# A graph-attention layer: the query projection moved from the prologue into the edge loop, ahead of the linear attention

## The reference

```
xn = layernorm(x)                                   # [6250, 256]
# 1. graph attention, 8 heads of 32, 206250 edges sorted by target node dst
q = xn @ Wq.T + bq;  k = xn @ Wk.T + bk;  v = xn @ Wv.T + bv
sim[e, h] = <q[dst[e]], k[src[e]]> / sqrt(32)
attn = softmax of sim over the edges of one dst
agg[d] = sum over its edges of attn * v[src[e]]
x1 = x + agg @ Wo.T + bo
# 2. linear attention over all nodes, 8 heads of 64
x1 += (q' @ (norm(k').T @ norm(v')) / N) @ w_out.T + b_out,   q', k', v' = xn @ w_qkv.T
# 3. a mixture of 8 experts of 1024 hidden units, each token goes to one expert
out = x1 + moe(layernorm(x1))
```

## Time and profile before

| | value |
|---|---|
| time, median of three runs | 2950.68 us |
| profiled execution: its span | 2949.1 us |
| busy share of the span: PE, DVE, ACT, POOL | 72%, 82%, 34%, 72% |
| matmuls, DVE instructions, POOL instructions | 9400, 3296, 2220 |
| granted TensorE clock, mean of the span | 0.875 |
| mean share of the 16 DMA engines, POOL's queue / SP's queue | 57.4% / 11.2% |
| first and last gather of `kv_d` rows begin | 272.61 and 2382.17 us |

### The profile page before, as it was taken

How to read it: one execution, slowest core, us unless ns; L and a number is a source line. 1 busy time by engine, 2 the same in 40 slices (tenths; PEclk the granted TensorE clock), 3 DMA queues, 4 the chain that set the end, 5 groups by cost and what they waited for, 6 DMA issues and landing times. The chain is left out here.

```text
span 2949.1 us, 36213 instructions
## 1 busy us (share of the span) xinstructions
PE 2127.7 (72%) x9400; PEld 1712.6 (58%) x9401; DVE 2429.0 (82%) x3296; ACT 1010.5 (34%) x4314; POOL 2119.7 (72%) x2220
## 2 busy tenths in 40 slices
PE   5675777767776777767888876556666655599998
PEld 4473555555565666555666554444444435599997
DVE  5676788888888999999999888899999985366665
ACT  3220555556566666611111111011111114345353
POOL 4465777777777777777777777777777775567785
PEclk9796888998999999989999898887888885599999
DMA  6746777777777777788888887777777758423331
GB/s 218 246 156 172 208 210 208 207 211 217 219 218 219 218 219 218 227 233 241 257 255 257 254 241 213 212 211 211 211 211 211 211 162 288 152 70 76 88 92 15
DMA packets 257830, 587.19 MB, mean 199 GB/s; under 512 B 49410, under 2 KB 135505, under 8 KB 257565
## 3 DMA queue, kind: packets, MB, share of 16 engines
q0 software_dynamic: 150480, 467.10, 57.4%
q1 hardware_dynamic: 97947, 109.47, 11.2%
q10 hardware_dynamic: 9296, 9.44, 0.9%
HBM read 519.05 MB, written 71.76 MB: 200 GB/s over the span
## 5 line engine op out<-in xcount | busy, mean ns | idle before, releaser
L1041 POOL DMA_INDIRECT wide<-kv_d,arena x1099 | 1051.0, 956 | 335.0 <-issue 326.7
L1340 PE MATMUL ps<-wide,arena 128*128 128x264 f32 x2432 | 694.6, 448 | 238.9 <-DVE wide L1444 238.6
L1340 PEld LDWEIGHTS ps<-wide,arena 128*128 128x128 f32 x2432 | 530.2, 223 | 395.2 <-DVE wide L1444 283.4
L1041 POOL DMA_INDIRECT arena<-kv_d,arena x539 | 515.3, 956 | 164.3 <-issue 159.1
L1176 ACT ACTIVATE ps<-wide 128x256 f32 x229 | 88.8, 388 | 1324.2 <-DVE arena L1410 1282.5
L1413 DVE TENSOR_REDUCE arena<-arena 128x64 f32<-128x2048 f32 x229 | 523.5, 2286 | 7.9
L1340 PE MATMUL ps<-arena 128*128 128x264 f32 x1216 | 350.4, 451 | 128.7 <-DVE arena L1444 128.7
L1410 DVE TENSOR_TENSOR arena<-wide,ps 128x2048 f32<-128x2048 f32 x153 | 349.3, 2283 | 105.7 <-DMA wide<-kv_d,arena 105.6
L1340 PEld LDWEIGHTS ps<-arena 128*128 128x128 f32 x1216 | 267.0, 225 | 209.0 <-DVE arena L1444 152.9
L1444 DVE TENSOR_TENSOR wide<-wide,ps 128x2112 f32<-128x2112 f32 x152 | 356.8, 2347 | 24.4 <-ACT arena L1191 24.4
L141 PE MATMUL ps<-halves 128*128 128x256 f32 (+2 forms) x2304 | 361.9, 319 | 3.2 <-DVE halves L1703 1.6
(11 more groups left out here) (310 smaller groups left out, 3137.8 us busy)
## 6 DMA issues: line engine op xcount, KB each, us to landing
wide<-kv_d,arena POOLq DMA_INDIRECT x1099, 3.8
arena<-in_w SPq DMA_DIRECT2D x16, 1024.0 KB, 5.4
kv_d<-wide SPq DMA_DIRECT2D x49, 260.0 KB, 2.2
arena<-xn_d SPq DMA_DIRECT2D x82, 128.0 KB, 3.4
arena<-kv_d,arena POOLq DMA_INDIRECT x539, 3.8
hb_d<-arena SPq DMA_DIRECT2D x16, 516.0 KB
q_d<-wide SPq DMA_DIRECT2D x49, 128.0 KB, 2.7
xn_d<-arena SPq DMA_DIRECT2D x7, 896.0 KB, 9.0
```

The costliest lines, as they stand in the source:

```text
L1041: e.indirect_dma_start(out=kvb[k][:, j, :], out_offset=None, in_=kv_d, in_offset=bass.IndirectOffsetOnAxis(ap=ixb[k][:, j:j + 1], axis=0)) ...
L1340: m = e.matmul(psE[(k + 1) % 3][:, 0:264], ident, kvb[b][:, j, 256:ROW], start=(j == 0), stop=(j == J - 1))
```

## The change

The projection of the queries leaves the prologue. In its place:

- the raw rows of `x` are copied from DRAM to DRAM into `row_d` (6250 rows of 256 numbers, `[0:N, 0:256]`), which also holds the neighbour lists (columns 256 to 319) and, in columns 320 and 321, each row's scale and offset of the layer norm, stored by `store_stat` once per group of seven tiles;
- POOL's sorted gathers (L600 for the first 13 tiles, L1171 for the other 36) bring rows of `row_d`, 322 numbers wide, instead of `q_d`. The first 13 no longer wait for the stores of k, v and q but for the lists and the scales (`t_rn`);
- `LEAD` = 3 tiles are turned into queries in straight code behind `grant`; the first eight rounds of the edge loop, 48 chunks (`CONV`), turn the other tiles into queries, one per chunk: ACT scales and shifts (`centered`), PE transposes (`turned`), ACT copies, PE multiplies (`queried`), ACT scales and writes the tile over the gathered one, SP stores it to `qs_d`. `mix`, `join` and `aux` follow behind these 48 chunks;
- the weight in the prologue has 512 columns instead of 768, and the tables are made for 294 instead of 300 chunks.

The work per tile in the prologue, and the release of the gathers (in the code T is PE, V DVE, S ACT, G POOL and Y SP; `wait(engine, tokens)` makes that engine wait):

```diff
-                    b0, b1_ = ps[2 * (u % 2)], ps[2 * (u % 2) + 1]
+                    b0 = ps[2 * (u % 2)]
                     wait(T, t_lo[u], t_bias.get(u - 2), t_W)
-                    for b_, c0, n in ((b0, 0, 512), (b1_, 512, 256)):
-                        m = product(b_[:, 0:n], [(xq[u % 2][:, i, k * 128:(k + 1) * 128], w[:, k, c0:c0 + n]) for k in range(2)
-                                                 for i, w in ((0, wh), (0, wl), (1, wh))])
+                    m = product(b0[:, 0:KV], [(xq[u % 2][:, i, k * 128:(k + 1) * 128], w[:, k, :]) for k in range(2)
+                                              for i, w in ((0, wh), (0, wl), (1, wh))])
...
+        s_xr, s_wq = sem("s_xr"), sem("s_wq")
+        dma(Y, row_d[0:N, 0:256], x, s_xr)
...
+        def store_stat(grp, tok):
+
+            wait(Y, tok)
+            return dma(Y, row_d[grp * 896:(grp + 1) * 896, 320:QI].rearrange("(t p) c -> p t c", p=128), stat[:, grp, :, :], s_rn)
...
-            while not t_kv:
+            while not t_rn:
                 yield
+            while fetching[0] is not None:
+                fetch_some()
             assert t_own_
-            wait(V, t_hz, *t_own_, *t_kv)
-            t_q49 = v(V.memset(qi[:, NT, :], 0.0))
-            wait(G, t_q49, t_ds, *t_own_, *t_kv)
+            wait(V, t_hz, *t_own_, *t_rn)
+            t_q49[0] = v(V.memset(qi[:, NT, :], 0.0))
+            wait(G, t_q49[0], t_ds, t_xr, *t_own_, *t_rn)
             for c in range(FIRST_Q):
-                (s_q0 if c < RING else s_q).inc(G.indirect_dma_start(out=qi[:, c, :], out_offset=None, in_=q_d,
-                                                                     in_offset=bass.IndirectOffsetOnAxis(ap=permS[:, c:c + 1], axis=0)), 16)
+                t_q[c] = s_q[c].inc(G.indirect_dma_start(out=qi[:, c, :], out_offset=None, in_=row_d,
+                                                         in_offset=bass.IndirectOffsetOnAxis(ap=permS[:, c:c + 1], axis=0)), 16)
```

The straight code behind `grant`, and the loops:

```diff
+        def centered(eng, tile):
+            return eng.activation(cxn, tile[:, 0:256], ACT.Identity, bias=tile[:, 321:322], scale=tile[:, 320:321])
+
+        def turned(eng):
+            eng.transpose(ct_ps[:, 0:128], cxn[:, 0:128], ident)
+            return eng.transpose(ct_ps[:, 128:256], cxn[:, 128:256], ident)
+
+        def queried(eng):
+            for k in range(2):
+                eng.matmul(cq_ps, cxT[:, k, :], wq[:, k, :], start=(k == 0), stop=False)
+            return eng.matmul(cq_ps, ones[0:1, :], bq_row, start=False, stop=True)
+
+        c_t, c_c, c_q, c_v = {}, {}, {}, {}
+        for n in range(LEAD + 4):
+            t = n - 2
+            if 0 <= t < LEAD:
+                wait(S, c_q[t])
+                m = S.activation(qi[:, t, 0:256], cq_ps, ACT.Copy, scale=32.0 ** -0.5)
...
+                else:
+                    m.then_inc(e_cv, 1)
+                    Y.wait_ge(e_cv, 1)
+                t_qs = dma(Y, qs_d[t * 128:(t + 1) * 128, :], qi[:, t, 0:256], s_qs)
+            t = n - 1
+            if 0 <= t < LEAD + 1:
+                wait(S, c_t[t], c_q.get(t - 1))
+                c_c[t] = a(S.activation(cxT, r3(ct_ps, 128), ACT.Copy))
+                wait(T, c_c[t], c_v.get(t - 1), t_wq, t_bq)
+                m = queried(T)
...
             e.reg_load(cnt_, nsl[0:1, 62:63])
-            e.reg_add(cnt_, cnt_, -(MIX + 2 + AUX))
-            if early is not None:
+            e.reg_add(cnt_, cnt_, -(CONV + MIX + 2 + AUX))
+            with turns(CONV):
                 for k in range(RING):
-                    body(k, mix=True, i=k)
-                with turns(Q_TURNS, True):
-                    for k in range(RING):
-                        early(k)
-                        body(k, mix=True, i=k)
-            with turns(MIX if early is None else MIX - 1 - Q_TURNS, True):
+                    body(k, conv=True)
+            before()
+            with turns(MIX, True):
                 for k in range(RING):
                     body(k, mix=True, i=k)
...
+            def convert():
+
+                e.reg_add(cn, cn, 1)
+                e.wait_ge(e_cq, cn)
+                e.wait_ge(e_ct, cn)
+                e.activation(qsf[:, bass.ds(val(e, qo, NT * QI), 256)], cq_ps, ACT.Copy, scale=32.0 ** -0.5).then_inc(e_cv, 1)
+                e.activation(cxT, r3(ct_ps, 128), ACT.Copy).then_inc(e_cc, 1)
+                e.reg_add(cv, cv, 1)
+                e.wait_ge(e_cv, cv)
+                centered(e, qsf[:, bass.ds(val(e, xt, NT * QI), QI)]).then_inc(e_cx, 1)
```

More of the change, by code:

```diff
@@ L30 @@
 AUX = 8
-CH = 300
-QI = 320
-WIDE = 50 * QI + 4 * J * ROW
+CH = 294
+QI = 322
+KV = 512
+CONV = 8
+LEAD = 3
+WIDE = 50 * QI + 4 + 4 * J * ROW
 WAIT_ROWS = 21
@@ L302, in inverse_root, with root, offsets @@
             return a(S.activation(o, o, ACT.Exp, scale=-0.5))
-        def root(n):
+        def root(grp):
             wait(S, (sv, sv.n))
[L306 to L320, removed]
-        wait(V, t_x[0])
-        t_n = {(0, 6): norm(xbuf[0], 7)}
+            return inverse_root(stat[:, grp, :, 0], r3(mv, 2)[:, :, 1])
+        def offsets(grp, tok):
+            wait(V, tok)
+            return v(V.scalar_tensor_tensor(out=stat[:, grp, :, 1], in0=r3(mv, 2)[:, :, 0], scalar=-1.0, in1=stat[:, grp, :, 0],
+                                            op0=ALU.mult, op1=ALU.mult))
+        wait(V, t_x[0])
+        spread(xbuf[0], range(7))
+        t_nm = {0: offsets(0, root(0))}
+        wait(V, t_nm[0])
+        for i in range(7):
+            t_n0 = v(V.tensor_scalar(out=xbuf[0][:, i, :], in0=xbuf[0][:, i, :], scalar1=stat[:, 0, i, 0:1], scalar2=stat[:, 0, i, 1:2],
+                                     op0=ALU.mult, op1=ALU.add))
+        t_n = {(0, 6): t_n0}
+        store_stat(0, t_nm[0])
         NB13 = 13
@@ L868, in gps_layer_kernel @@
         e_xw = [esem(f"xw{i}") for i in range(3)]
-        e_qt = [esem(f"qt{i}") for i in range(RING)]
+        e_qt = [s_q[RING + 1 + i].h for i in range(RING)]
+        e_cx, e_ct, e_cc, e_cq, e_cv = [esem(n) for n in ("cx", "ct", "cc", "cq", "cv")]
+        e_cs = [esem(f"cs{i}") for i in range(RING)]
         assert FIRST_Q + RING * Q_TURNS == NT
@@ L913, in aligned, with rounds @@
             return nc.Fori(0, end, engines=(kind,))
-        def rounds(e, pre, body, step, between, aux=AUX, kind=None, early=None):
+        def rounds(e, pre, body, step, between, aux=AUX, kind=None, before=None):
             def turns(end, hint=False):
@@ L976, in _, with query_out @@
             e.wait_ge(s_xn.h, s_xn.n)
-            used, w = regs(e, "y_", ["used", "w"], [2, 0])
+            used, w, made, to = regs(e, "y_", ["used", "w", "made", "to"], [2, 0, 1, LEAD * 128])
+            for k in range(RING):
+                e.nop().then_inc(e_cs[k], 16)
+            def query_out(k):
+                e.reg_add(made, made, 1)
+                e.wait_ge(e_cv, made)
+                e.dma_start(qs_d[bass.ds(val(e, to, 48 * 128), 128), :],
+                            R1[:, bass.ds(val(e, at, 48 * QI), 256)]).then_inc(e_cs[k], 16)
+                e.reg_add(to, to, 128)
+                e.reg_add(at, at, QI)
+            (at,) = regs(e, "y_", ["at"], [LEAD * QI])
+            with aligned(e, mybir.EngineType.SP, (NT - LEAD) // RING):
+                for k in range(RING):
+                    query_out(k)
+            for k in range((NT - LEAD) % RING):
+                query_out(k)
             def mix_in(i):
@@ L1209, in last_out, with stored @@
                 base_out(RING - 1)
[L1211 to L1216 removed]
+            def stored():
+                e.wait_ge(e_ct, CONV * RING + 1)
+                for k in range(RING):
+                    e.wait_ge(e_cs[k], 16 * ((NT - LEAD - 1 - k) // RING + 2))
+            rounds(e, "a_", body, join, (first_out, last_out), AUX - 1, mybir.EngineType.Activation, stored)
             for _ in range(2):
@@ L1325, in record, with body @@
                 e.load([f_], tabF[:, bass.ds(val(e, cg, CH - 14) * TW + 2, 1)])
-            def body(k, mix=False, join=None, aux=False, i=0):
+            def body(k, mix=False, join=None, aux=False, i=0, conv=False):
                 b = (k - 1) % RING
@@ L1351, in body @@
                     base_of(k)
-            rounds(e, "t_", body, join, (first_base, lambda: None))
+            rounds(e, "t_", body, join, (first_base, lambda: None), before=first_keys)
             for k in range(2):
```

196 lines of the change are left out of this document (123 added, 73 removed).

## The result

The changed kernel takes 2980.3 us (median of four runs, 2977.93 to 2980.51) against 2950.8 for the kernel before (a fourth run of it is in that median): a ratio of 1.0098, with a 95% interval of 1.0086 to 1.011. It is 29.5 us slower. The forecast was 2955, within 2940 to 2972; the time lies outside. The profiled span is 2979.3, 30.2 more than before.

A forecast was written before the change was run, and what follows sets the result against it. POOL's unbroken stream of gathers, 1.26 us each, was taken to bound the kernel. Prologue gains and the new lead-tile chain put its first gather 4.3 us later: 2949.1 + 4.3 = 2953.4, plus 1.6, 2955 us; range 2940 to 2972.

The forecast's parts named there:

- The frame: Edge loop: one unbroken POOL stream at 1.26 us per gather, unchanged in length; only the first gather's start moves, 4.3 us later.
- Rival (c): Edge loop: ACT's new mixing loop stalls at each of 16 turns, about +30 us, 2985; chance 0.08.
- step 1: Prologue up to tile 21: POOL's earlier gathers and the slower DMAs from the copy of x cancel: 0, between -3 and +3 us.
- the slack at tile 21: Before tile 21: DVE waits 6.76 us for gathered targets, taken to absorb most of tiles 3 to 9 standing some 10 us.
- Rival (b): Prologue: the copy of x costs double, 90 ns a piece, +20 us, 2975; chance 0.11 together with other prologue delays.
- tiles 21 to 43: Prologue, forecast as tiles 21 to 48: fewer bias adds and matmuls gain 12 us, bounds 8 and 20 to 27.
- step 2: Tiles 44 to 48: no separate term and no stall behind list stores priced; forecast only within the 12 us gain of tiles 21 to 48.
- tables and chain: Last tile to first gather: W0 22 us after tile 48, lead tiles 13.3 us, then SP's stores and index DMAs 8.0 us.

The follow-up runs named there:

- the mended copy in the kernel before: The kernel before with only the copy of x added, as 6240 and 10 rows into rows 1536 bytes apart: 2952.7 us, ratio 1.0008.

## Why the prediction was wrong, point by point

**The frame was right.** The edge loop is one stream of POOL's; converting, mixing 48 chunks later and 98% of DVE cost nothing, and the time moved by the first gather's shift to 0.7 us. Rival (c) didn't come: ACT's L1265 has 5.2 us of idle time put down to issue in the whole run, against single stalls of 7.5 before.

**Failed step 1: the prologue up to tile 21, forecast 0, measured +14.1.** The step priced the copy at 46 ns over 16 engines, 18 us, of which most was to be slack. It was 32.6 us: 10 engines, since 6250 isn't divisible by 16, and 55 ns a piece. The pieces and the mended copy in the kernel before show both. The forecast also let the stores of the first tiles queue and share; in the trace SP could not even issue the next DMA, so that nothing behind it moved. And the slack at tile 21 was not there: POOL's gathers of the targets are three per tile at most, so they stood for 21.3 us with tile 3, the last was issued at 112.0 instead of 95.5, and DVE waited for them for 8.35 us, more than the 6.76 before. The row on DVE's wait was read as slack, where it is a chain that starts with the same tiles. Rival (b) named the place and the point of decision rightly, at 2975 and 11 in 100 together with other delays, though for another reason: it doubled the price of a piece, where about 6 us came from the number of engines (33.4 against 27.1) and as many from the pitch (27.1 against 20.7). Its argument against, that the engines move 1 KB in 46 ns in either queue, was read from ACT's loads, and looked at the piece and not at the number of engines.

**Right: tiles 21 to 43.** The forecast had tiles 21 to 48 gain 12 us; tiles 21 to 43 gained 14.2.

**Failed step 2, not in the sum at all: tiles 44 to 48, +13.0.** Tile 44 waits behind the list stores in SP's queue: 13.9 us instead of 2.6, which is 11.4 of the 13.0. A pitch of 1288 bytes is worth 7.1 of it (21.1 against 14.0 us for tiles 44 to 48, in the two versions with pieces of 160 rows). 4.3 more are what the changed kernel took beyond the version with the index DMAs first, whose code is the same there (26.8 against 22.5); that stays open. The table steps that now stand between the last tiles cost little: with the pitch mended the stretch takes 14.0, against 13.8 before. The diff showed the 322; I priced the change of place of these stores, and not their shape.

**Right in place and near in size: tables and chain.** Tile 48 to the end of W0: forecast 22, measured 19.9. PE's granted clock was 0.50 from 278 to 293 us, the half level, as forecast; from W0 to ACT's third output 13.3 forecast, 278.1 to 292.4 = 14.3 measured; from there to the first gather 8.0 forecast, 10.4 measured, above all since POOL's start took 2.6 us behind the last index DMA's landing (298.5 + 1.7) and not 0.5. The index version shows that the chain and SP's stores held POOL: 23.4 us go with the order of SP's DMAs alone, and the one other wait that the trace names, DVE's clearing, is not in the way.

So 276.8 was forecast for the first gather and 302.8 measured: 14 of the 26 us by step 1, 11 by step 2 (13.0 less the 2.2 that tiles 21 to 43 gained beyond the forecast), 1 by the tables and the chain together.

## What to carry to other kernels

Ask of every new DMA over how many engines it goes, and price it by that number: with aligned rows 6250 rows moved 233 pieces per us and 6240 rows 330, 149 rows held SP for 8 us, and whatever stands behind such a DMA in the same queue waits. A row widened by two numbers changes the start of every row: the small stores into it took 15.7 us to land instead of 8.5. And where code is put in front of a block, look which later instruction of the same queue another engine is waiting for: three stores put behind the index DMAs were worth 23 us.

## What the runs showed of the hardware

- Behind a DMA from SP of 149 rows of 1 KB, SP's next issue takes 8.1 to 8.5 us; behind one of 160 rows it doesn't stand (0.33 us, first tiles). With 6250 rows the engines' share is 0.68 to 0.69 from 25 to 30 us, with 6240 rows 1.09 to 1.15.
- SP stands in the issue of a DMA of 22 rows for 32.6 us when one of 6250 rows is ahead of it. With 160 pieces of 40 KB ahead it doesn't stand, though those land only after 26.4 us.
- Pieces of 256 bytes (time of a packet, by the share of the queue): 19 to 20 ns at a row pitch of 1280 or 1536 bytes, 44 to 59 ns at 1288. Pieces of 1 KB from DRAM to DRAM: 46 ns (6250 rows) and 53 (6240) at 1536, 55 and 83 at 1288; 233, 330, 200 and 220 pieces per us.
